# A Mamba-style mixer between two routed feed-forward layers: two gate activations leave slots 9 and 40 of a batch for slots 13 and 46

## The reference

```
x = x + 0.5 * ffn(layernorm(x))      # 8 experts, tokens chosen per expert by a Sinkhorn gate
x = x + mixer(layernorm(x))
x = x + 0.5 * ffn(layernorm(x))
```

```
xr = x @ W_in.T;  x_ssm, res = xr[..., :512], xr[..., 512:]
x_conv = silu(conv1d(x_ssm, conv_w) + conv_b)          # 4 taps, causal
delta = softplus(x_conv)
h_t = exp(delta_t * A) * h_(t-1) + x_conv_t**2          # 16 states per channel
y_t = x_conv_t * sum over the states of h_t
out = (y * silu(res) + D * x_conv) @ W_out.T
```

## Time and profile before

| | |
|---|---|
| runs | 3545.2, 3546.92, 3549.64 us (median 3546.92) |
| the profiled execution | 3556.01 us |
| its span, first to last instruction | 3554.5 us |
| mean granted TensorE clock over the span | 0.869 of full speed |
| first scans of the 8 batches | 408.8, 730.5, 1042.1, 1352.8, 1663.4, 1974.0, 2284.6, 2595.2 us |
| ScalarE table loads at L1472, L1486 and L1522 | 32, 8 and 42 |

### The profile page before, as it was taken

How to read it: one execution, slowest core, us unless ns; L and a number is a source line. 1 busy time by engine, 2 the same in 40 slices (tenths; PEclk the granted TensorE clock), 3 DMA queues, 4 the chain that set the end, 5 groups by cost and what they waited for, 6 DMA issues and landing times. The chain is left out here.

```text
span 3554.5 us, 29882 instructions
## 1 busy us (share of the span) xinstructions
PE 2753.7 (77%) x9684; PEld 1514.2 (43%) x9684; DVE 3150.0 (89%) x2664; ACT 2099.4 (59%) x2219; POOL 1295.2 (36%) x871
## 2 busy tenths in 40 slices
PE   6303778899889889988988998898789677874555
PEld 4202333354346335434634543463345255433444
DVE  7996489999999999999999999999999968994555
ACT  6101568876877787687778768677866634221111
POOL 0003254437244443724444372444011110016665
PEclk8556899999899999989999998999899887885777
DMA  8103377788778778877877887787677669233342
GB/s 332 66 0 108 84 171 177 153 180 182 154 172 164 177 153 179 183 153 172 163 177 155 180 183 151 173 163 174 127 145 139 130 122 364 89 158 117 131 143 89
DMA packets 128024, 553.85 MB, mean 156 GB/s; under 512 B 19782, under 2 KB 55272, under 8 KB 79424
## 3 DMA queue, kind: packets, MB, share of 16 engines
q0 software_dynamic: 75168, 393.49, 53.1%
q1 hardware_dynamic: 52736, 158.94, 12.1%
HBM read 152.62 MB, written 117.45 MB: 76 GB/s over the span
## 5 line engine op out<-in xcount | busy, mean ns | idle before, releaser
L1312 DVE TENSOR_TENSOR_SCAN state<-state,drive 128x2048 f32<-128x2048 f32 x512 | 2223.7, 4404 | 51.0 <-ACT state L1518 50.9
L1518 ACT ACTIVATE state<-delta,neg_a 128x2048 f32<-128x2048 f32 x512 | 1018.8, 2005 | 216.8 <-DMA delta<-xc 84.0
L1769 PE MATMUL ps_states<-state,ident 128*128 128x512 f32 x1792 | 854.3, 622 | 78.7 <-DMA state<-state 64.3
L1193 POOL DMA_DIRECT2D state<-state x255 | 233.5, 916 | 1310.1 <-DVE state L1312 1286.4
L1671 PE MATMUL ps_proj<-x1t,w_in 128*128 128x512 f32 x1024 | 514.5, 648 | 84.7 <-ACT xc L1467 29.8
L1769 PEld LDWEIGHTS ps_states<-state,ident 128*128 128x128 f32 x1792 | 349.1, 201 | 482.0 <-issue 384.8
L1687 PE MATMUL ps_proj<-conv_in,tap 128*128 128x512 f32 x1024 | 488.7, 629 | 54.5 <-ACT conv_in L1431 33.9
L1122 POOL DMA_INDIRECT picked<-normed_rows,slot_now x112 | 353.5, 3157 | 100.5 <-PE ps_rows L1652 55.7
L1671 PEld LDWEIGHTS ps_proj<-x1t,w_in 128*128 128x128 f32 x1024 | 207.2, 207 | 369.2 <-issue 281.3
L1138 POOL DMA_INDIRECT x<-routed_rows,row_now x112 | 339.2, 3029 | 34.6 <-issue 34.6
L1687 PEld LDWEIGHTS ps_proj<-conv_in,tap 128*128 128x128 f32 x1024 | 204.3, 202 | 320.6 <-issue 280.8
(11 more groups left out here) (344 smaller groups left out, 3288.4 us busy)
## 6 DMA issues: line engine op xcount, KB each, us to landing
state<-state POOLq DMA_DIRECT2D x255, 1024.0 KB
delta<-xc POOLq DMA_DIRECT2D x24, 1024.0 KB
normed_rows<-rows_in SPq DMA_DIRECT2D x8, 2048.0 KB
x_rows<-x SPq DMA_DIRECT2D x16, 1024.0 KB
dense_rows<-dense_mid SPq DMA_DIRECT2D x16, 1024.0 KB
f_dense<-dense_rows SPq DMA_DIRECT2D x16, 1024.0 KB
rows_in<-in_x SPq DMA_DIRECT2D x7, 2048.0 KB
expert<-in_experts SPq DMA_DIRECT2D x56, 256.0 KB
```

The lines of the kernel that those rows point to most:

```text
L1193: nc.gpsimd.dma_start(out=state[held(q)][:], in_=state[held(q - 1)][:], accum_op=ALU.add).then_inc(pair_landed(b, q // 2)[0], 16)
L1312: nc.vector.tensor_tensor_scan(state[held(q)][:], state[held(q)][:], drive[j % 2][:], 0.0, ALU.mult, ALU.add).then_inc(state_ready, 1)
L1518: nc.scalar.activation(state[held(q)][:], delta[j % 2][:], ACT.Exp, scale=g.neg_a[:, j, n:n + 1]).then_inc(decay_ready, 1)
L1769: mm = nc.tensor.matmul(ps_sum[c][:], g.ident[:], state[held(q)][:, c * CH:(c + 1) * CH], start=(opening and n == 1), stop=(n == N - 1))
```

## The change

Two entries of `SILU` are split. The gate of unit 0 goes from slot 9 to slot 13, and the gate of unit 2 from slot 40 to slot 46; `activate` of units 1 and 3 stays in slots 9 and 40. As every slot of `SILU` ends in `both_tables`, and a Silu after an exp is preceded by a load, the two new slots have two table loads each. Nothing else is changed, on no other engine.

```
-    SILU = {9: ((0,), 1), 25: ((), 2), 35: ((1,), None), 40: ((2,), 3), 58: ((3,), 4)}
+    SILU = {9: ((), 1), 13: ((0,), None), 25: ((), 2), 35: ((1,), None), 40: ((), 3), 46: ((2,), None), 58: ((3,), 4)}
```

## The result

The kernel became slower: 3581.06 us in the median of four runs (3580.63 to 3584.26) against 3546.06 in four of the kernel before; the ratio is 1.0104, with an interval of 1.0086 to 1.0123. That is 35.0 us by the medians. The forecast was 3588 in a range of 3556 to 3607, on the right side and 7 us too long. The two profiled executions differ by less, 3581.29 against 3556.01, because the one of before took longer outside the mixer. From the start of the first scan to the end of the last the mixer took 2484.1 us before and 2517.1 after, **33.0** more; what lies around it took 1071.9 and 1064.2. I compare mixers.

What follows compares the result with a forecast made beforehand. VectorE sets the pace, with TensorE setting it up to `combine`; 30.0 us (slot 13) plus 11.2 (slot 46) make 41 on 3556.0, so 3597, or 3588 as a median (the profiled execution was 9.1 above); range 3556 to 3607.

Steps and rivals of the forecast that it cites:

- The stall of step 16: TensorE before step 16, batches 1 to 6: waits 3.3 us for ScalarE's late read_bank of slot 14.
- The working by slack: At slot 14, read_bank ends 4.19 us later; TensorE's step 16 had 0.99 us to spare, so it stalls 3.3 us.
- The clock's 1.7 us at this site: TensorE behind step 16, batches 1 to 6: lower granted clock after the idle adds 1.7 us (bounds 0 and 3.0).
- My first rival: Both TensorE stalls occur, but the granted clock does not fall: +19 us, 3566; chance 0.20.
- The place of the wait: VectorE, per batch: 0.9 us at scan 14, and some 5.8 us instead of 1.8 at `combine` for TensorE.
- Slot 46: Unit 2's gate at its new place, batches 0 to 6: delays less the waits saved, 11.2 us in all.
- The idle ahead of the third chunk: TensorE's projections after slot 47's copy: third chunk starts 1.8 us late, with some 3.5 us idle before it.
- at most 1.0 us of the 1.75 is left: Scan 47: the delayed decay leaves VectorE at most 1.0 us of the 1.75 us saved at scans 43 and 44.
- The clock behind the idle: TensorE's projections from the third chunk on: lower granted clock adds 1.7 us a batch (bounds 0 and 3.0).
- the waits of 43 and 44 vanish: Scans 43 and 44: decays come in time, so VectorE's waits of 0.62 and 1.13 us go, 1.75 us.
- The rival in which the gain at 43 and 44 decides: No TensorE delay reaches VectorE; 1.0 us per batch is left at scan 47: 7 us faster, 3540; chance 0.08.
- The drain behind a load: ScalarE: about 1.38 us behind each table load would make the time about 36 us later; chance 2%.

Runs made afterwards that it cites:

- Slot 14: The kernel before with only unit 0's gate moved, from slot 9 to slot 14: ratio 1.0001 (0.9989 to 1.0013).
- r3 first: The kernel before with unit 0's gate in slot 13 and TensorE's output rows r3 taken ahead of step 16: ratio 0.9996 (0.9986 to 1.0006).
- the gate without loads: The changed kernel with an exp for the Silu in slots 13 and 46, so no table loads there: ratio 0.9996 against the kernel before.
- slot 48: The kernel before with only unit 2's gate moved, from slot 40 to slot 48: ratio 0.9974 (0.9959 to 0.9990).
- slot 51: The kernel before with only unit 2's gate moved, from slot 40 to slot 51: 3532.31 us against 3545.76, ratio 0.9964.

## Why the prediction was right, step by step

**The stall of step 16** was forecast as 3.3 us in batches 1 to 6; it is 3.13 in five and 3.05 in the sixth. The working by slack (0.99 us to spare, a handover 4.19 late) holds. The profile names L1396, the copy of the picked rows, as what it waited for, where I named L1402; both stand behind the gate in slot 13, and L1402's end, at 1432.22 in batch 3, is the later one, 0.10 us ahead of step 16:

```profile
1431.47 0.38 ACT L1396 COPY picked_t<-ps_rows 128x256 f32<-128x256 f32 x1
1431.73 0.49 ACT L1402 ACTIVATE routed<-ps_rows,gate_now 128x256 f32<-128x256 f32 x1
```

Slot 14, r3 first, and the gate without loads each take the stall away, or all but 0.3 us of it, in their own manner, and with it the cost of this site; so the wait is shown to be the cause.

**The clock's 1.7 us at this site is the term that was mis-sized.** I added it in all six batches. It measures 1.6 to 1.7 (45.65 us instead of 44.05 from step 16 to the end of r7, for the same 145 products) in batches 2, 3 and 5 alone. Batches 3 and 4, with the granted clock third from the right:

```profile
1432.32:1477.97 45.65, 45.65 (x145) 30.88 (x146) 40.06 (x10) 24.82 (x22) 26.25 (x17) 0.96 0.84 166
1749.23:1793.28 44.05, 44.05 (x145) 29.96 (x146) 40.06 (x10) 24.84 (x22) 29.24 (x16) 1.00 0.83 164
```

In batches 2, 3 and 5 part of it is given back: the low stretch at the batch's start ends 2.6 to 2.9 us behind scan 0 instead of 3.7. In batches 1, 4 and 6 the clock stays up behind step 16, and the low stretch at the batch's start runs until 4.6 or 4.7; in batch 1 it did so before, too (4.8). At half speed 1 us of that is worth 0.5 us, so r7 should end 3.13 + 0.5 = 3.6 us later in batches 4 and 6, 3.1 in batch 1, and 3.13 + 1.7 - 0.5 = 4.3 in the others. Measured from scan 0, each batch against itself before, it ends 3.8 and 3.7, 3.2, and 4.2 to 4.3 us later, not 5.0. The step that failed is that I added the two losses to a batch that was otherwise as before; its start gives and takes as well. VectorE waits 21.9 us more in the six batches; the forecast was 30.0. My first rival, that the clock stays up, holds in half of the batches.

**The place of the wait** was forecast as 0.9 us at scan 14 and 5.8 at `combine`, 6.7 in all. It is 5.2 to 5.9 in all, and in three parts: 0.1 to 1.5 at scan 14, 0.8 or 2.4 at `gate` behind scan 19, and 3.25 or 3.3 at `combine`. I had taken `gate` in slot 19 for free, since its own input from ScalarE comes earlier; it also takes TensorE's sums, and those are behind step 16. Batch 0, costed at 0, lost 1.8 here and got 1.6 back at its start.

**Slot 46** was forecast at 1.6 us a batch, 11.2 in all; it cost 14.8. The idle ahead of the third chunk is 3.4 us in six of the seven batches, where I had 3.5. Waits appear at scan 50, as forecast, and at 47, where 0.74 us is what "at most 1.0 us of the 1.75 is left" comes to. Two terms that I set alike in all batches differ from one to the other. The clock behind the idle, taken as 1.7, costs 0.1 in batches 0, 3 and 5, 1.8 in batch 2 and 2.9 in batches 1, 4 and 6 (3.70, 5.40 and 6.5 us for eight products, against 3.60 for eight of the same size in the earlier trace rows). And that the waits of 43 and 44 vanish is right in batches 1, 4 and 6 alone; in the other four 1.2 to 1.4 us are left. A batch with 0.1 of the one and 1.3 of the other (3 and 5) lost 1.5 us here, one with 2.9 and none (1, 4 and 6) 2.2 to 2.8, and batch 2, which has both, 3.0. Slots 48 and 51 show that the delays behind the gate, and not its work, are the cost. The rival in which the gain at 43 and 44 decides is borne out by slot 51 in the main; in slot 48 the waits at scans 41 to 54 are only 1.0 us shorter than before, of the mixer's 4.8.

**Between the sites** 7.1 us came back that I had not looked for. In batches 1 to 6 the wait at scan 34 went from 1.8 or 1.9 us to 1.1 in batch 3, and to 0.4 to 0.6 in the others. From 41.2, the two errors at the sites (-8.1 and +3.6), these -7.1, and +3.4 of small things (VectorE's own 3.2, and batches 0 and 7) give the 33.0. That the total came closer than its terms is luck: they erred to both sides.

**The loads.** There are 32 more, as forecast, but 16 are at L1486 (8 before, 24 after) and 16 at L1522 (42 to 58), none more at L1472: `activate` in slots 9 and 40 now loads for itself. Each takes 1.283 us, and the next activation starts within 0.02 us (1595.77 + 1.28 = 1597.05, and the Silu at 1597.06). The drain behind a load, of which the Trainium skill speaks on its page "ScalarE: Activation LUTs", section "What ACT_TABLE_LOAD costs", isn't seen, and the 36 us that it would have added did not come.

## What to carry to other kernels

Before an operation is moved within one engine's list, look up which copies stand behind its new place and which engine takes them next in order: the gate of unit 0 cost 17 us in slot 13 and nothing in slot 14, and the gate of unit 2 cost 6 to 8 us in slot 46 and gained 13 in slot 51 (12 and 11 by the mixers). An engine that works without a gap cannot make up for a late input, even if it isn't busiest over the whole run: here TensorE had 0.99 us to spare at step 16, and the rest of the delay came out at VectorE. A wait can also be cured on the other side, by giving the waiting engine its next ready work first.

## What was not expected of the hardware

TensorE's low stretches belong to a rhythm of the whole batch. Before, batches 2 to 6 were alike in length to 0.15 us, each with its low stretches in the same places (batch 6 with one more); with batches 5 us longer the places and lengths differ from batch to batch. What VectorE waits later goes with them. Two stretches of after show it, ahead of scan 42 in batch 3 and at the same place in batch 4:

```profile
1553.20:1559.80 6.60, 5.51 (x7) 2.44 (x8) 6.60 (x8) 6.60 (x6) 0.00 (x0) 0.50 0.00 0
1869.00:1872.40 3.40, 3.31 (x8) 1.62 (x9) 3.40 (x4) 3.40 (x3) 0.00 (x0) 1.00 0.00 0
```

In batch 3 the granted clock is 0.50 here for the whole stretch, the convolution's chunk comes late, and ScalarE waits 1.38 us for it in slot 40, ahead of `activate`:

```profile
1562.29 0.58 ACT L1438 COPY delta<-ps_proj 128x512 f32<-128x512 f32 x1
1564.25 0.59 ACT L1438 COPY delta<-ps_proj 128x512 f32<-128x512 f32 x1 [1.38 <-PE ps_proj L1687]
1564.85 1.28 ACT L1486 ACT_TABLE_LOAD   x1
```

The waits of scans 43 and 44 are then still there, with the gate out of slot 40. In batch 4 the clock is up, and they are gone. The same goes for slot 51: 1.4 us are left in batches 2, 4 and 6, where the low stretch here is 6.8 us long, and under 0.1 in 1, 3 and 5, where it is 3.4. In batches 1 to 6 of all ten profiled kernels ScalarE waits 1.0 to 1.7 us in slot 40 behind a stretch of 6.8 us, and under 0.1 behind a short one or none. With the gate in slot 40 the waits up to scan 44 are 1.6 to 1.8 us after a short stretch or none and 2.7 to 3.2 after a long one. At scan 34 the wait is 1.1 to 1.9 us after a low stretch of about 7 us and 0.3 to 0.7 after one of half that length. All of this goes together in the traces, but what sets where the stretches fall was not tried.
